# First norm on ScalarE, and powers, scalings, logits and sigmoid put ahead of splits and copies, in a gated block with a routed feed-forward

## The reference, cut to what matters

```python
def _layernorm(x, eps=1e-05):
    return (x - mean(x)) / sqrt(var(x) + eps)

def _smooth_quant_linear(x, w):            # s smooths columns, then rows are scaled to 127 and rounded
    s  = max(sqrt(max(amax_col|x|, EPS) / max(amax_col|w|, EPS)), EPS)
    xs, ws = x / s, w * s
    x_scale, w_scale = max(amax_row|xs|, EPS) / 127, max(amax_row|ws|, EPS) / 127
    return round(xs / x_scale) @ round(ws / w_scale).T * x_scale * w_scale.T

h = _smooth_quant_linear(_layernorm(x), gate_up_weight)
y = _smooth_quant_linear(silu(gate) * up, down_weight)
x = x + tanh(g_xattn) * y

z = _layernorm(x)
bids = sigmoid(z @ conf_W.T + conf_b) * wealth      # top 2 of 8, softmax of the two
for e in range(8):
    g = z @ base_gate + z @ gate_A[e] @ gate_B[e] * SCALING
    u = z @ base_up   + z @ up_A[e]   @ up_B[e]   * SCALING
    o = silu(g) * u
    out += we[e] * (o @ base_down + o @ down_A[e] @ down_B[e] * SCALING)
x = x + tanh(g_ffn) * out
```

## Time and profile before

| what | us |
|---|---|
| median of 3 runs | 272.02 (271.61 to 274.47) |
| the profiled execution | 274.34 |
| its span, first to last instruction | 272.2 |
| TensorE busy | 237.7 (87%) |
| VectorE busy | 193.4 (71%) |
| ScalarE busy | 176.6 (65%) |
| GpSimd busy | 136.8 (50%) |

### The profile page before, as it was taken

How to read it: one execution, slowest core, us unless ns; L and a number is a source line. 1 busy time by engine, 2 the same in 40 slices (tenths; PEclk the granted TensorE clock), 3 DMA queues, 4 the chain that set the end, 5 groups by cost and what they waited for, 6 DMA issues and landing times.

```text
span 272.2 us, 4997 instructions
## 1 busy us (share of the span) xinstructions
PE 237.7 (87%) x1550; PEld 216.7 (80%) x1550; DVE 193.4 (71%) x411; ACT 176.6 (65%) x382; POOL 136.8 (50%) x152
## 2 busy tenths in 40 slices
PE   0756386699996999999998999999999999999883
PEld 0646274488986998889987999999999999998772
DVE  2968968887718981347687778777777777777664
ACT  2238679898764645668998676666666666666450
POOL 4396672774952011158754544894555555531151
PEclk9977869689999999999999999999999999999999
DMA  5944423437798349636318245455444545440544
GB/s 150 342 134 109 116 73 97 109 122 219 250 295 282 135 159 316 232 98 213 124 69 280 86 161 173 154 176 193 175 174 170 172 163 170 159 166 29 168 162 154
DMA packets 31348, 45.78 MB, mean 168 GB/s; under 512 B 14104, under 2 KB 25760, under 8 KB 31328
## 3 DMA queue, kind: packets, MB, share of 16 engines
q0 software_dynamic: 4416, 21.50, 23.3%
q1 hardware_dynamic: 20752, 14.03, 18.8%
q10 hardware_dynamic: 6160, 9.98, 10.3%
HBM read 33.57 MB, written 11.93 MB: 167 GB/s over the span
## 4 chain that ended last, share of the span: by engine, by line
PE 51%; DVE 16%; DMA 13%; POOL 8%; issue 5%; ACT 4%; SPq 1%; DVEq 0%; ACTq 0%; POOLq 0%
PE pY L56 6%; PE pY L58 5%; PE pY L60 5%; DMA xin<-normed,tok 4%; PE pT L1801 4%; POOL held_B L603 3%; DMA x_resid<-in_x_dram 2%; PE bank L56 2%; PE bank L58 2%; PE bank L60 2%; PE pG L1790 2%; PE pG L1791 2%; PE pU L1791 2%; PE pU L1790 2%; DMA raw<-in_L_ffn_down_A_dram 2%
## 5 line engine op out<-in xcount | busy, mean ns | idle before, releaser
L56 PE MATMUL pY<-Wd_hi,hT_hi 128*128 128x320 f32 (+1 forms) x126 | 42.0, 333 | 0.1
L60 PE MATMUL pY<-Wd_hi,hT_lo 128*128 128x320 f32 (+1 forms) x126 | 39.7, 315 | 0.0
L58 PE MATMUL pY<-Wd_lo,hT_hi 128*128 128x320 f32 (+1 forms) x126 | 39.6, 315 | 0.0
L567 POOL DMA_INDIRECT bin<-base_products,tok x18 | 24.8, 1376 | 22.9 <-DVE hbuf L1370 21.6
L559 POOL DMA_INDIRECT xin<-normed,tok x19 | 18.4, 971 | 32.5 <-DVE share L1313 15.8
L573 POOL DMA_INDIRECT results<-yb,dest x17 | 16.9, 992 | 24.6 <-ACT yb L909 23.4
L741 ACT COPY brow<-bank 128x448 f32<-128x448 f32 x32 | 16.9, 531 | 14.8 <-PE bank L60 14.3
L1380 DVE TENSOR_TENSOR hT_lo<-pT,hT_hi 128x512 fp32r<-128x512 f32 (+1 forms) x38 | 23.5, 620 | 3.2 <-ACT hT_hi L886 2.3
L56 PE MATMUL bank<-Wbase_hi,x2T_hi 128*128 128x448 f32 x64 | 24.6, 385 | 1.0 <-ACT brow L741 1.0
L56 PEld LDWEIGHTS pY<-Wd_hi,hT_hi 128*128 128x128 f32 x126 | 23.8, 189 | 0.7 <-ACT Wd_lo L875 0.5
L58 PEld LDWEIGHTS pY<-Wd_lo,hT_hi 128*128 128x128 f32 x126 | 23.8, 189 | 0.0
(11 more groups left out here) (329 smaller groups left out, 715.3 us busy)
## 6 DMA issues: line engine op xcount, KB each, us to landing
base_products<-brow ACTq DMA_DIRECT2D x16, 448.0 KB, 3.1
yr<-results SPq DMA_DIRECT2D x8, 256.0 KB, 5.6
raw<-in_L_ffn_gate_B_dram SPq DMA_DIRECT2D x8, 224.0 KB, 2.5
raw<-in_L_ffn_up_B_dram SPq DMA_DIRECT2D x8, 224.0 KB, 3.3
raw<-in_L_ffn_down_A_dram SPq DMA_DIRECT2D x7, 256.0 KB, 5.1
x_resid<-in_x_dram SPq DMA_DIRECT2D x4, 256.0 KB, 5.2
q<-in_fside_BxS2xS_dram ACTq DMA_DIRECT2D x4, 256.0 KB, 7.0
normed<-q ACTq DMA_DIRECT2D x4, 256.0 KB, 3.7
```

The lines of the kernel that those rows point to most:

```text
L56: m.matmul(outs[i], hi, whi[i], start=first, stop=False, skip_group_check=True)
L58: m.matmul(outs[i], hi, wlo[i], start=False, stop=False, skip_group_check=True)
L60: ins = m.matmul(outs[i], lo, whi[i], start=False, stop=last, skip_group_check=True)
L567: g.indirect_dma_start(out=bin_[:, (j + 1) % 2].rearrange("p a i -> p (a i)"), out_offset=None, in_=gun, in_offset=bass.IndirectOffsetOnAx ...
```

## The change

The first norm moves from VectorE to ScalarE. GpSimd now also negates the mean and multiplies it by the power, so that ScalarE forms `x * rstd + (-mean * rstd)` as an Identity activation with scale and bias. Each `rstd_of` has four GpSimd instructions where it had two, in place in `mv`. The calls `x_norm(0)` to `x_norm(3)` leave VectorE and stand at three places of ScalarE's program.

Other calls change place. On GpSimd `roots(0)` goes ahead of the first `lo`. On TensorE `x_T1(0)` goes ahead of `w_T(1)`, and `logits(3)` ahead of `unit(9)`. On VectorE `deq1(1)` goes ahead of `smooth2(0)`. On ScalarE `scale2(3)` and `c_row(2)` go ahead of a `split`, `x2_hi(3)` ahead of `resid(3)`, and the sigmoid ahead of `unit_out(9)` and two `split`s.

```diff
 def rstd_of(b):
     pool.wait_ge(s_var, b + 1)
-    vs = mv[:, TB * b:TB * (b + 1), 1]
+    ms, vs = mv[:, TB * b:TB * (b + 1), 0], mv[:, TB * b:TB * (b + 1), 1]
     g.tensor_scalar(vs, vs, LN_EPS, None, ALU.add).then_inc(s_eps, 1)
-    pool.wait_ge(s_eps, b + 1)
-    g.tensor_tensor(rstd[:, TB * b:TB * (b + 1)], vs, expo[:, 0:1].to_broadcast([P, TB]), ALU.pow).then_inc(s_rstd, 1)
+    g.tensor_scalar(ms, ms, -1.0, None, ALU.mult).then_inc(s_eps, 1)
+    pool.wait_ge(s_eps, 3 * b + 2)
+    g.tensor_tensor(rstd[:, TB * b:TB * (b + 1)], vs, expo[:, 0:1].to_broadcast([P, TB]), ALU.pow).then_inc(s_eps, 1)
+    pool.wait_ge(s_eps, 3 * b + 3)
+    g.tensor_tensor(ms, ms, rstd[:, TB * b:TB * (b + 1)], ALU.mult).then_inc(s_rstd, 1)
...
 rstd_of(2)
-lo(1)
 roots(0)
-lo(4)
+lo(5)
 roots(1)
...
+def x_norm(b):                                  # ScalarE
+    act.wait_ge(s_rstd, b + 1)
+    for t in range(TB * b, TB * (b + 1)):
+        a.activation(q1[:, b, t % TB, :], xs_all[:, t, :], ACT.Identity, scale=rstd[:, t:t + 1],
+                     bias=mv[:, t, 0:1]).then_inc(s_xn, 1)
+
 a.activation(warm[:, :], expo[:, 1:2], ACT.Silu).then_inc(s_warm, 1)
+x_norm(0)
 a.dma_start(cW[:, :], conf_W).then_inc(d_cW, 16)
 for b in range(NB):
     a.dma_start(q2[:, b, 2:4, :], cv[:, b]).then_inc(d_c[b], 16)
+x_norm(1)
+x_norm(2)
...
 w_row(0)
+x_norm(3)
 scale(1)
...
 q2T_out(2)
-split(1)
 scale2(3)
 c_row(2)
+split(1)
 resid(1)
...
 unit_out(7)
+x2_hi(3)
 resid(3)
-split(1)
-x2_hi(3)
-split(1)
+split(2)
 unit_out(8)
-unit_out(9)
-split(1)
 act.wait_ge(s_logit, 1)
 a.activation(bids[:, :, :], bids[:, :, :], ACT.Sigmoid).then_inc(s_sig, 1)
-split(1)
+unit_out(9)
+split(2)
...
 stats(2)                                        # VectorE
-x_norm(0)
 w_max(0)
 w_recip(0)
-x_norm(1)
-x_norm(2)
 x_max(0)
...
 smooth(1)
-x_norm(3)
 deq1(0)
...
 quotient(3)
+deq1(1)
 smooth2(0)
-deq1(1)
...
 w_T(0)                                          # TensorE
+x_T1(0)
 w_T(1)
-x_T1(0)
...
 unit(8)
-unit(9)
 logits(3)
-for u in range(10, 14):
+for u in range(9, 14):
     unit(u)
```

More of the change, by code:

```diff
@@ L1047, in reciprocals @@
                 link(v.tensor_scalar(low, rc, EPS, EPS * EPS, ALU.mult, ALU.max))
[L1049 to L1053, removed]
             def x_max(b):
```

## The result

The changed kernel takes 270.72 us in the median of 20 runs (269.32 to 274.09). In 20 runs beside it the kernel before took 273.82 (271.61 to 275.84), 1.8 above the three runs that the forecast started from. The ratio is 0.990, 95% interval 0.9878 to 0.9922: 2.7 us faster (2.1 to 3.3), about half of the 5.4 forecast. The profiled execution took 270.51 us with a span of 268.3, 3.8 us faster than the profiled one of before.

The account below looks back on a forecast made before the run. From about 87 us the kernel is a rigid body around TensorE; ahead, an engine-hopping chain has avoidable waits. 2.7 + 1.4 + 0.1 + 1.2 = 5.4 us off 274.34 gives 268.9, less 2.32 to the median: 266.6, range 264.2 to 270.8.

Parts of the forecast that it names:

- Part A: Front, batch 0: norms on ScalarE and an earlier power start smooth(0) at 15.5 instead of 18.19, gaining 2.7 us.
- Part D: Router: earlier logits and sigmoid free VectorE at about 78.6 instead of 81.26; 1.2 us arrive at the rank products.
- would end at 14.65, or 15.15: Front: VectorE's 3.04 us between quotient and smooth(0) ends at 14.65, or 15.15 if it waits for c_T(0).
- Part B: Batch 3's norm: without x_norm(3) on VectorE, deq1(0) and all that follows come 1.4 us earlier, hidden on ScalarE.
- Part C: VectorE's deq1(1) ahead of smooth2(0) fills a wait of 1.73; between 0 and 0.4, taken as 0.1 us.
- late load: Rival at the front: cW and ctx land 7.0 us after issue, total gain 1.9 us, 270.1; chance 0.12.
- ScalarE no bound: Rival that ScalarE becomes the bound: its eight activations are exposed, 1.6 us slower, 273.6; chance 0.06.
- Absorbed: Rival: weight splits, low parts and transfers from 57 us keep their times; only 1.2 us left, 270.8; chance 0.12.

Follow-up runs that it names:

- lo_wait: Changed kernel with GpSimd's first low parts held back until smooth(0) has begun; 271.02 us, ratio 0.989.
- router_only: Kernel before with only the router's moves: last logits ahead of unit 9, x2_hi(3) and sigmoid earlier on ScalarE; 273.83 us, ratio 0.999.
- sigmoid_only: Kernel before with only ScalarE's router moves: sigmoid and x2_hi(3) ahead of the splits, logits still behind unit 9; 272.92 us, ratio 0.998.
- logits_only: Kernel before with only the last logits moved ahead of unit 9, sigmoid still behind the splits; 275.93 us, ratio 1.009.
- recip_logits: Changed kernel with w_recip(1) behind smooth(0) and the last logits behind unit 9 again; 270.89 us, ratio 0.989.
- best: Changed kernel with w_recip(1) behind smooth(0), last logits behind unit 9, and 64 unread transposes filling TensorE's idle places; 271.70 us, ratio 0.992.
- recip_late: Changed kernel with the second group of weight reciprocals, w_recip(1), set behind smooth(0) on VectorE; 270.89 us, ratio 0.988.

## Why only half of the predicted gain came

Two parts of the sum failed, A and D. **Part A**, the front (2.7), missed most. Its transfers and TensorE were as forecast: `factors(0)` at 14.50 against 14.2, no wait for a transfer, 1.06 long against 1.3. What failed is the sentence that VectorE's own work "would end at 14.65, or 15.15" as before. It took the length of that work from a trace in which GpSimd stood at the power during `w_recip(1)`; the change put the power earlier and so five low parts beside it. The two stretched steps took 1.37 instead of 0.34. lo_wait shows this: without that neighbour the steps are short and `smooth(0)` starts at 15.62.

Each stretched step ends 0.03 behind the end of a low part (16.78 against 16.75 here), so it waits until that GpSimd instruction is through:

```profile
15.62 1.13 POOL L491 TENSOR_TENSOR Wbase_lo<-raw,Wbase_hi 128x448 fp32r<-128x448 f32 x1
15.95 0.83 DVE L1057 TENSOR_SCALAR low<-rc 128x6 f32<-128x6 f32 x1
```

The prediction knew such waits, at part D, but only for steps with two inputs in SBUF, the on-chip memory that VectorE and GpSimd share. These steps have one. The Trainium skill, "SBUF — State Buffer", section "SBUF: two separate sides", names a second kind of VectorE instruction that excludes a GpSimd one for its whole length, that in a 2-port perf mode. The trace agrees as to the whole length: TENSOR_SCALAR went from 0.17 to 0.83, and RECIPROCAL between two such steps stayed at 0.19. Which mode these steps ran in, no run shows.

A second error lies in the reading of before. Of four profiles with the first 18 us of before, the shown one was the latest: `smooth(0)` at 18.19 against 17.56, 17.10 and 17.19 (router_only, sigmoid_only, logits_only), because its factors took 2.08 against 1.16 to 1.60. Six profiles with the changed front have it at 16.62 in the mean (15.73 to 16.95), so part A is worth 0.9 there. And `smooth(0)` was the wrong mark: lo_wait, recip_logits and best have it 1.2 to 1.9 earlier than the changed kernel, and none has a `smooth(1)` earlier by more than 0.01, or a shorter mean. At `smooth(1)` the same profiles give 1.1 for part A (25.73 in the four of before, 24.63 in the six).

**Part B** (1.4) was right: 1.5 in the profiles between `smooth(1)` and `deq1(0)`, 1.4 +-0.7 in the times, hidden on ScalarE as said. The Trainium skill's rule in "ScalarE: Activation LUTs", section "Rules for kernel authors", wants plain multiplications and additions on VectorE. Two norms took 0.70 there in a clear place against 1.09 on ScalarE, as the rule has it; beside the low parts they took 2.22, and there the measurement decides against it.

**Part C** (0.1) was right in size, 0.03 at equal clock. That the changed profile loses 0.7 between `deq1(0)` and `smooth(3)` goes with TensorE's half clock at `q1_T(2)` and `factors(3)`, which the prediction didn't weigh.

**Part D** (1.2) was right in the profile (1.7 between first unit and rank products, no wait for picks, unit 12's wait down from 1.04 to 0.16) and wrong in the times (0.3 +-0.8). The sigmoid came 4.4 earlier, not 6.5, as the parts ahead of it had given less. Its place was priced rightly: 1.2 in the profiles. Three picks took 0.81, 1.12 and 1.22 beside low parts, where 0.22 is usual, as the prediction's rule says; but two had done so before (1.25 and 0.96), and the picks were still ready just before TensorE came to the rank products. The step that failed is the early logits, which were taken to cost nothing. Moved ahead of unit 9, they sometimes go with half clock in units that no longer have a wait to hide it (1.4 each time). How many executions meet that stretch is not known; 4 of 8 profiles with both edits did.

The sum as measured: A 1.0 (what the others leave, not measured by itself), B 1.4, C 0, D 0.3, together 2.7. The rivals did not come: no late load, ScalarE no bound. *Absorbed* is not shown: the kernels whose front was made still earlier got nothing for it, but there the gain was gone by `smooth(1)`, ahead of the weights that this rival is about. The forecast of 266.6 was also 1.8 too low for its base of three runs.

Open is how much of the remaining scatter is the clock's. Each result gives the span and the mean granted clock of every execution, hence twice the span times (1 - clock) as us at half clock. Within a kernel one such us goes with 0.11 us of time (+-0.04) in 106 executions of before, and with 0.19 (+-0.05) in 89 of the changed kernel and eight variants. This fits a change that took out waits behind which the clock could hide; but fillers that hold the clock gain nothing, so it is a correlation and not a cause shown.

## What to carry to other kernels

When a step is moved, cost also what takes its old place beside the other engines: here the power left and low parts came to stand beside VectorE's reciprocals. Read a gain at the next point where an engine had been waiting, not at the step that was moved. Split a two-part edit: of the router's two moves one gains in the profiles, and the other gains nothing and, alone, loses 2.3 us.

## What the runs showed of the hardware

- VectorE's small TENSOR_SCALAR of 128x6 takes 0.17 us alone and 0.54 to 0.83 in the changed kernel (1.13 in best) beside a GpSimd subtraction of 128x448. Beside GpSimd's power of 128x4 (1.01 us) it keeps its 0.17 (before, at 15.21). Two norms of 128x256 take 0.70 or 2.22. TENSOR_REDUCE from the matmul banks and RECIPROCAL beside the same low parts keep their 0.68 and 0.19.
- In the stretch from 30 to 35 us the same instructions ran at a mean granted clock of 0.63 in one execution and 1.00 in another; eight transposes and eight factors took 3.3 us at the lower clock of the first.
- In recip_late TensorE is idle for 0.6 us, makes a row of 8-column matmuls and goes on to the units; then the clock falls to half for 3.4 us, in which matmuls of 448 columns take 0.57 instead of 0.36, though TensorE never stops. The changed kernel's own profile has the same idle time and row, and no fall.
